# Layer-1 attention: global projections grouped by array shape over both banks, and the fill of a local pair placed between mask and values

## The reference

```python
x = x + global_latent_attn(rmsnorm(x, norm1_w), g_wq, g_kv_down, g_k_up, g_v_up, g_wo)
x = x + local_gqa_attn(rmsnorm(x, norm2_w), l_wq, l_wk, l_wv, l_wo)
```

## Time and profile before

| what | value |
|---|---|
| median of 3 runs | 2338.94 us (2335.61 to 2344.2) |
| the profiled execution | 2335.73 us, span 2334.0 us, mean granted TensorE clock 0.976 |
| PE busy | 2152.2 us (92%) in 15812 instructions |
| PE weight loads busy | 1410.4 us (60%) |
| DVE, ACT, POOL busy | 1449.2 (62%), 1209.5 (52%), 1046.7 us (45%) |
| values matmuls L1863 | 2688 passes, 206.7 us busy |
| scores matmuls L1832 | 896, 173.6 us busy, 27.5 us idle before them |

### The profile page before, as it was taken

One profiled execution on the slowest core, in us unless ns is written; L12 is line 12 of the kernel. 1 busy time (PEld: TensorE's weight loads), 2 busy tenths in 40 slices (PEclk: granted clock), 3 DMA queues, 4 the chain that ended last, 5 costly groups with the idle time before them and its releaser, 6 DMA issues. The chain is left out here.

```text
span 2334.0 us, 41144 instructions
## 1 busy us (share of the span) xinstructions
PE 2152.2 (92%) x15812; PEld 1410.4 (60%) x15812; DVE 1449.2 (62%) x3302; ACT 1209.5 (52%) x1796; POOL 1046.7 (45%) x982
## 2 busy tenths in 40 slices
PE   6999999999999999999999999599999988887797
PEld 4555565556555565558888888434444455566567
DVE  5687758776687758764656666456545555556523
ACT  4555535554465535542333333378777766654533
POOL 2777757777577757783323223333332311110001
PEclk9999999999999999999999999699999999999999
DMA  2000000000000000021000000000000000002001
GB/s 77 2 1 1 1 2 1 1 1 1 1 1 1 1 1 2 1 46 30 1 1 1 1 1 1 0 1 1 1 1 1 1 1 2 2 12 69 1 1 37
DMA packets 36197, 18.17 MB, mean 8 GB/s; under 512 B 16666, under 2 KB 33828, under 8 KB 36004
## 3 DMA queue, kind: packets, MB, share of 16 engines
q1 hardware_dynamic: 36004, 15.54, 2.6%
HBM read 13.44 MB, written 2.10 MB: 7 GB/s over the span
## 5 line engine op out<-in xcount | busy, mean ns | idle before, releaser
L318 POOL TENSOR_TENSOR a_first<-a_first,a_ring 128x512 f32<-128x512 f32 (+3 forms) x352 | 557.7, 1584 | 254.0 <-PE a_o_ps L542 216.9
L1963 ACT ACTIVATE g_probsT<-g_s_ps 128x1024 f32<-128x1024 f32 (+2 forms) x448 | 369.0, 869 | 136.4 <-PE g_s_ps L1832 82.6
L676 ACT ACTIVATE a_ring<-a_st 128x768 f32<-128x768 f32 (+1 forms) x256 | 228.7, 918 | 85.9 <-PE a_st L527 84.2
L773 DVE TENSOR_REDUCE a_part_max<-a_mx 128x2 f32<-128x1024 f32 x128 | 156.5, 1222 | 131.5 <-PE a_mx L490 130.2
L796 DVE RECIPROCAL a_row_inv<-a_row_inv 128x256 f32<-128x256 f32 x128 | 218.6, 1732 | 24.0 <-ACT a_row_inv L664 24.0
L542 PE MATMUL a_o_ps<-a_ring,a_v 128*64 128x512 f32 (+3 forms) x1280 | 226.4, 474 | 1.5 <-POOL a_ring L300 1.4
L1243 ACT ACTIVATE m_silu<-m_up,m_b 128x512 f32<-128x512 f32 x160 | 109.8, 689 | 216.4 <-PE m_up L1178 215.0
L1863 PE MATMUL g_o_ps<-g_probsT,g_values 128*32 128x512 f32 (+5 forms) x2688 | 206.7, 419 | 5.2 <-POOL g_probsT L1708 5.1
L1832 PE MATMUL g_s_ps<-g_qT,g_kT 64*128 64x512 f32 (+3 forms) x896 | 173.6, 435 | 27.5 <-ACT g_probsT L1963 21.8
L1708 POOL TENSOR_SCALAR_AFFINE_SELECT g_probsT<-g_probsT 128x512 f32<-128x512 f32 x128 | 88.5, 695 | 244.8 <-ACT g_probsT L1963 244.6
L490 PE MATMUL a_mx<-a_k_hi,a_q_hi 64*128 64x512 f32 (+3 forms) x768 | 147.0, 404 | 24.6 <-DVE a_largest L780 17.1
(11 more groups left out here) (344 smaller groups left out, 4274.5 us busy)
## 6 DMA issues: line engine op xcount, KB each, us to landing
m_w<-in_L_ffn_rw SPq DMA_DIRECT2D x2, 1024.0 KB, 9.0
s_w<-in_L_ffn_w SPq DMA_DIRECT2D x1, 2048.0 KB, 8.9
s_w<-in_L_ffn_w SPq DMA_DIRECT2D x4, 512.0 KB, 9.7
out_x<-x SPq DMA_DIRECT2D x8, 256.0 KB, 2.3
m_w<-in_L_ffn_rw SPq DMA_DIRECT2D x2, 512.0 KB, 6.0
x<-in_L_attn_x SPq DMA_DIRECT2D x2, 256.0 KB, 2.9
a_outT<-in_L_attn_w_k SPq DMA_DIRECT2D x1, 512.0 KB, 4.5
a_outT<-in_L_attn_w_q SPq DMA_DIRECT2D x1, 512.0 KB, 5.4
```

The lines of the kernel that those rows point to most:

```text
L318: pool.tensor_tensor(total[:, h, q:q + w], total[:, h, q:q + w], probs_of(n, u)[:, h, off:off + w], ALU.add).then_inc(added, 1)
L676: act.activation(probs_of(n, u)[:, :, 0:w], st_ps[u % 2][:, :, 0:w], ACT.Exp).then_inc(exp_done, 1)
L773: last = dve.tensor_reduce(part_max[:, i, :], mx_ps[:], AX.X, ALU.max)
L1963: act.activation(out, src.rearrange("p k (j n) -> p k j n", j=at_once), ACT.Exp, scale=float(HD) ** -0.5).then_inc(exp_done, 1)
```

## The change

In global rounds a half of the projections (four blocks of tokens, two banks) is issued at once: first the query matmuls of both banks, then the latent ones of both. `fill_banks` takes the uses of two steps in one call, and callers call it once a pair. In `local_pair` it is called before the late values, no longer behind them.

```diff
-                def project(k, x, quarter):
+                def projected(k, quarter):
+                    return [(x_ps[k % 2][:, i * 256:i * 256 + 192], slice((quarter * 2 + i) * P, (quarter * 2 + i + 1) * P))
+                            for i in range(2)]
+
+                def project_local(k, x, quarter):
                     x_read(pe, "input", x, 0, quarter // 2)
-                    if not is_local(x):
-                        x_read(pe, "latent", x, 0, quarter // 2)
-                    for i in range(2):
-                        blk = quarter * 2 + i
-                        out = x_ps[k % 2][:, i * 256:i * 256 + 192]
-                        rows = slice(blk * P, (blk + 1) * P)
-                        if is_local(x):
-                            last = pe.matmul(out, normedT[:, rows], w_in[1][:], start=True, stop=True)
-                        else:
+                    for out, rows in projected(k, quarter):
+                        last = pe.matmul(out, normedT[:, rows], w_in[1][:], start=True, stop=True)
+                    last.then_inc(x_filled, 1)
+
+                def project_global(k, x, half):
+
+                    x_read(pe, "input", x, 0, half)
+                    for two in range(2):
+                        bank_free(k + two)
+                        for out, rows in projected(k + two, 2 * half + two):
                             pe.matmul(out[:, 0:D], normedT[:, rows], w_in[0][:, 0:D], start=True, stop=True)
+                    x_read(pe, "latent", x, 0, half)
+                    for two in range(2):
+                        for out, rows in projected(k + two, 2 * half + two):
                             last = pe.matmul(out[:, D:], latT[:, rows], w_up[:], start=True, stop=True)
-                    last.then_inc(x_filled, 1)
+                        last.then_inc(x_filled, 1)
...
                 def fill_banks(r, n):
-                    for k in uses_at(r, n):
+                    for k in uses_at(r, n) + uses_at(r, n + 1):
                         _, _, what, x, i, half = USES[k]
+                        if what == "project" and not is_local(x):
+                            if half == 0:
+                                project_global(k, x, i)
+                            continue
                         bank_free(k)
...
                     mask_scores(r, n)
                     mask_scores(r, n + 1)
+                    fill_banks(r, n)
                     late_r, late_n = (r, n - 2) if n else (r - 1, STEPS - 2)
                     if is_local(late_r):
                         weigh_all(late_r, late_n)
                         weigh_all(late_r, late_n + 1)
                     else:
                         weigh_last_of(late_r, late_n)
-                    fill_banks(r, n)
-                    fill_banks(r, n + 1)
```

More of the change, by code:

```diff
@@ L1807, in fill_banks @@
                         elif what == "project":
-                            project(k, x, 2 * i + half)
+                            project_local(k, x, 2 * i + half)
                         elif what == "back":
@@ L1903, in local_pair @@
                         weigh_last_of(late_r, late_n)
-                    fill_banks(r, n)
-                    fill_banks(r, n + 1)
-                for n in range(STEPS):
+                for n in range(0, STEPS, 2):
                     fill_banks(-1, n)
```

## The result

| kernel | median | runs | profiled execution (span) |
|---|---|---|---|
| before | 2341.15 us | 7 | 2335.73 (2334.0) |
| after | 2349.98 us (2347.89 to 2351.6) | 7 | 2347.89 (2346.2) |

The ratio is 1.0039, 95% interval 1.0028 to 1.0051: 9 us slower, clear of noise, and just under the 0.5% that the prediction took as its bound. The forecast was 2355 and slower by more than that. The direction is as forecast; the step is a little over half of the +16.4 us of the sum, or, against the 2341 of the longer series of the kernel before, 9 for 14.

The account below looks back on a forecast made before the run. TensorE's own time was taken to bound global pairs with a projection fill, and a loop through ScalarE's second exponent the changed local pairs; -8.0 + 24.4 = +16.4 us gave 2355, range 2340 to 2367.

Parts of the forecast that it names:

- the +16.4 us of the sum: Whole kernel: -8.0 us from grouped projections plus +24.4 us from the fill ahead of the values in local pairs.
- The row of the output projection: Global projections: eight output projection passes of the query passes' shape take 1.09 us; their 0.11 spacing gave 1.03 for latent passes.
- the half-price: Global projections, low end: latent passes at 0.055 us each, half of 0.11, giving about 0.75 us for eight.
- the 0.16 us bound: Global projections, high end: latent passes at 0.16 us each, giving 1.32 us for eight.
- Part 1: Grouped projections: 6.0 us saved in rounds 0 to 2 and 2.0 in the lead-in, -8.0 us (-4.5 to -11).
- The loop: Local pairs: first values, second exponent, second score, masks, values again; with the fill inside, 3.23 us against 2.79 for eight transposes.
- The walk through a local round: Added waits pair by pair in a local round with later values: 7.1 us a round, 21.3 over rounds 4 to 6.
- the cover: Local pairs 14 to 20: a 16.8 us VectorE chain ending in 2.70 us TensorE idle hides later values; otherwise 2.5 us more.
- Fewer switches as the winner: Rival: TensorE's own time decides in local pairs, -8.0 - 8.6 = -16.6 us, 2322; chance 0.07.
- Cancelled: Rival: the loop costs half, local +12 to +15, grouping -8 or more, no change, 2342 to 2348; chance 0.15.
- Slower still: Rival: idle time brings the 1.2 GHz clock into local rounds, or VectorE's cover breaks; +35, 2374; chance 0.08.
- Grouping gains nothing: Rival: ScalarE takes the grouped projections' time back in the next pair; +24, 2363; chance 0.1, counted as slower.

Follow-up runs that it names:

- fourth place: The changed kernel with a fourth place for local probabilities in free columns of the same tiles, so step n's exponent waits for values of n-4: 2332.07 us, ratio 0.9967.

## Why the prediction was right or wrong

**Grouping, inside the rounds: right.** 2.12 us a half against 2.1 forecast, with the latent passes at the 1.03 that was taken between two far ends. Undisturbed rounds are 2.0 us shorter each. The row of the output projection was the right neighbour, the half-price and the 0.16 us bound were both off. The Trainium skill's rule (TensorE: Matmul & The Clock Gate, section The mechanism), that a weight load overlaps running matmuls only where the row group differs, would have left 0.16 us between latent passes; they all use one row group, and 1.03 us for eight and the way out doesn't fit it. The same section also lets a load into a background weight buffer go ahead, which no run here tells apart.

**Grouping, the lead-in: mis-sized.** Two halves were forecast to save 2.0 us (1 to 3). From the first projection pass to the end of the last they took 8.31 us before and 4.99 after, 3.3 us less (and 6.73 in the one profile without grouping that had less of the low clock there), and from that first pass to the first scores 31.8 and 28.5 us; the means of four profiles without grouping and eight with it are 31.6 and 28.7. The wait for ScalarE was there, 0.35 us for 0.5 forecast. What was missed is that the second half no longer falls at the low clock, where it was in the kernel before:

```profile
1487.31 0.69 PE L1778 MATMUL g_x_ps<-g_w_up,g_part 32*128 32x64 f32 x2
...
1484.71 1.13 PE L1782 MATMUL g_x_ps<-g_w_in,g_normedT 128*128 128x128 f32 x8 [0.35 <-ACT g_values L1952]
1485.77 1.10 PE L1786 MATMUL g_x_ps<-g_w_up,g_part 32*128 32x64 f32 x8
```

The first row is of the kernel before (0.43 us for the same two passes in the first half), the others of the kernel after. The start of the first scores alone, counted from the start of the span, shows 2.0 us (means 1513.2 and 1511.2), since the work ahead of the lead-in varies by more than that.

**Grouping as a whole: mis-sized.** "Part 1: -8.0 us (-4.5 to -11)" measured -10 and -13. The term left out is the granted clock, in the rounds and in the lead-in: the sum priced the change at the high clock and took the stretches at the low one as they were in one profile.

**The loop: right.** 3.23 and 3.66 us a pair were forecast and are what the trace shows in every round, in the pairs that wait for nothing else; the second exponent follows the values by 0.61 us, ScalarE idles 0.94 us for a forecast of 0.8. TensorE idles 0.3 us and not 0.5 in front of the second score: the busy time of a score group that stands alone is 0.41 us, and 0.31 behind another.

**The walk through a local round: right in sum, off in several places.** Pairs 0 to 4 were 11.42 us in round 6, 11.40 forecast, but 12.37 in round 5: there the 1.55 us in which TensorE waited for VectorE was followed by matmuls at the low clock, and in round 6 the same wait was not. Timelines of PE in the kernel after, round 5, then round 6:

```profile
1942.65 1.12 PE L1748 MATMUL g_x_ps<-ident,g_q_slots 128*128 128x128 f32 x4 [1.55 <-DVE g_att L2027]
1943.70 1.30 PE L1875 MATMUL g_o_ps<-g_probsT,g_values 128*32 128x160 f32 x24
...
2006.46 0.66 PE L1748 MATMUL g_x_ps<-ident,g_q_slots 128*128 128x128 f32 x4 [1.54 <-DVE g_att L2027]
2007.05 0.76 PE L1875 MATMUL g_o_ps<-g_probsT,g_values 128*32 128x160 f32 x24
```

Pair 12 was put at +1.0 and pairs 14 to 20 at nothing; the five together took +0.5 to +0.7. VectorE's rotation began 4.25 us behind pair 12's mask in round 4 (4.6 forecast), and the chain from there to the scores of pair 22 was 16.8 us long again (1897.56 to 1914.39). So the cover held: TensorE's wait at its end fell from 2.70 us to 2.01. Pairs 24 and 26, put at +1.6, took +1.25, +2.6 and +1.3 in rounds 4 to 6. At the round's end +0.8 was +0.6. Rounds 4 to 6 came out 7.2, 8.6 and 5.2 us longer for about 7 each, and round 7 3.5 for 3.7.

The stage as a whole came out at 24.4 us over in the first pair of profiles and at 24.2 between the means of four with the fill ahead (232.4) and four with it behind the values and three places (208.2), for a forecast of 24.4. That it agrees so closely is in part luck: single rounds miss by up to 2 us, mostly with where the low clock fell, and these misses cancel.

**The tail: missed.** The sum has no term for what follows the last mask, and it gave 2 us back: 244.1 to 244.5 us in the four profiles with the fill ahead and three places, 246.0 to 247.9 in the four with it behind the values. The last half of the outputs is transposed once VectorE has copied it, and that copy queues behind the residual of the batch before. In the kernel before it was late by 1.86 us, and matmuls at the low clock followed, as TensorE's timeline shows:

```profile
2092.34 1.08 PE L1748 MATMUL g_x_ps<-ident,g_outT 128*128 128x128 f32 x4 [1.86 <-DVE g_outT L2028]
2093.22 2.13 PE L1748 MATMUL g_x_ps<-ident,g_att 128*128 128x128 f32 x8
```

In the slower local rounds of the kernel after VectorE had mostly caught up:

```profile
2105.15 0.63 PE L1748 MATMUL g_x_ps<-ident,g_outT 128*128 128x128 f32 x4 [0.65 <-DVE g_outT L2038]
2105.70 0.63 PE L1748 MATMUL g_x_ps<-ident,g_att 128*128 128x128 f32 x4
```

The shorter wait, 1.9 us in all four profiles of the one kind and 0.6 in all four of the other, is 1.2 us of the 2. The clock is a weaker ground for the rest: in the second profile of the kernel before the four transposes behind a wait of 1.87 us took their usual 0.63 and the next four 0.67, and only later ones were slow, yet this stretch was the longest of the eight, 247.9 us. So the rest of the 2 us is not shown.

Put together from the means: -2.9 lead-in, -10.9 and +0.9 global rounds, +24.2 local, about -2 tail, +9 us; measured +8.8 and +10.5. The mechanism of the forecast held, and its loss was right; the gains beside it were some 7 us short, and so +16.4, over 0.5%, became 0.4%.

**The rivals.** Fewer switches as the winner holds for a single pair once the wait is gone: with a fourth place a pair takes 2.64 us, where "some 0.16 us" less than 2.79 was put down for it. It does not hold for the stage, 211.8 us against 206.5 with values first, for the sake of pairs 0 to 4; it took a choice of pairs to earn it. Of the drain that the Trainium skill states (TensorEngine Tiling (Array Packing), Key Properties) the runs show a price, 0.15 us for a change of shape less (2.79 to 2.64) and 0.14 for one more (2.79 to 2.93), earned only where TensorE ends the pair. "Cancelled" came near in total, for another reason than it gave: not a shorter loop but a larger gain in front of it. "Slower still" did not come: TensorE idles 0.33 us in such a pair, and the low clock was granted for 20.5 us of the local stage, for 17.1 before. "Grouping gains nothing" is refuted.

## What to carry to other kernels

Before work is moved behind or ahead of other work on a queue, list who waits for what is pushed back, including waits that now cost nothing: a gap of 0.07 us that stands in every pair can be a loop that is nearly closed, and whatever is put inside it is paid beyond its slack. Here 0.87 us went between mask and values (0.65 to 1.52), the slack was 0.43 (a pair of 2.79 us for a loop of 2.36), and the pair paid 0.44. A rotation of buffers that was just deep enough for one order isn't for another; here unused columns of the same tiles gave the fourth place, and turned a loss of 0.4% into a gain of 1% together with a choice, pair by pair, of which work goes first. And find a pair in the trace in which the cover is already missing, as the pairs without a fill are: it shows the period that the change will give.

## What the runs showed that was not expected

Grouping matmuls by shape came with less time at the low clock in rounds 0 to 2, 13.3 us for 25.6 on the mean of eight profiles and of four, and that was worth nearly as much as the passes saved (10.9 us in all, 6 of them by the passes). One profile of the eight had no less than the least of the four, and the cause is open.

And a wait of TensorE can cost more than its length, but its length doesn't tell. In the kernel after, the matmuls behind 1.55 us in round 5 and behind 2.01 us in round 5 took 1.7 to 2.1 times their usual durations; behind 1.54 us in round 6 they took the usual ones, and so did the first scores behind 2.01 us there (0.41 us for two passes). Behind 1.86 us at the end of the local rounds the kernel before was slow at once in one profile and, behind 1.87, not at once in the other. Where such stretches fall differs from one execution of a program to the next, so a single pair of profiles is no measure of a change of a few microseconds.
